# Attention and mixture-of-experts block: P*V of two key tiles together at every second key tile

## The chip, the cores and the metric

The kernel runs on one core of a Trainium2 chip. The time is the device time of one execution in microseconds (us), taken as the median of several runs of the same program. The trace that is read here comes from one profiled execution of the kernel before the change.

## What is computed

The reference is a transformer block on x of 2048 tokens by 256 features: normalise, attention with 16 heads, normalise and add, then a router with 16 experts of which each token takes two, a shared expert, normalise and add. Only the attention is touched. Cut to what matters:

```python
q = (x @ wq); kva = x @ wkv_a; ckv = rmsnorm(kva[..., :64]); k_pe = rope(kva[..., 64:])
k_nope, v = split(ckv @ wkv_b)              # 16 heads
scores = einsum('bhqd,bhkd->bhqk', qs, ks) * scale
scores = where(causal, scores, min)
attn = softmax(scores, axis=-1)
out = einsum('bhqk,bhkd->bhqd', attn, v)    # P*V
y = out.reshape(b, s, H * VD) @ wo
```

The kernel folds wkv_b into the query weights and into wo, so that keys are 128 wide (64 latent and 64 rotary values, the same for all heads) and values are the 64 latent values.

## The kernel before

**Tiling.** Queries are worked in four chunks of 512 (`qc` 0 to 3; here called stages 0 to 3), keys in tiles of 128. Stage `qc` has KT = 4(qc+1) key tiles: 4, 8, 12, 16. The 16 heads are worked in 8 pairs `p`; the two heads of a pair are `s` 0 and 1. A *unit* `i = 2*kt + s` is one head's 128 keys by up to 512 queries, in transposed form; the last four key tiles of a stage lie on the diagonal and have 512, 384, 256 and 128 columns. A pair has U = 2*KT units.

**One unit of scores** (`score_unit`) is three TensorE matmuls in fp16 (lines 1202 to 1204, high and low parts), a fourth (line 1362) that subtracts the row maximum where `row` holds, and one for the causal mask on the diagonal (line 1364). In stages 0 and 1 both heads take the fourth; in stages 2 and 3 only head 0 does, and for head 1 VectorE adds the negated maximum in place (`shift`, line 854). ScalarE then takes the exponential into `Pr` (line 525), a ring of 8 units in SBUF, and GpSimd adds the units up into `Pacc` for the softmax sums (lines 388 and 395). The scores stand in a ring of 4 PSUM banks.

**P*V** (`values(p, kt)`, line 1386) is one fp32 matmul for each head of the pair; each is two passes, so a key tile shows as four instructions. Head 0 writes the lower 64 partitions of one PSUM bank and head 1 the upper 64, all key tiles of a pair adding up there. It waits for the exponentials of its two units; ScalarE may overwrite a slot of `Pr` when P*V and GpSimd have read it.

**Looking ahead.** While pair p is worked, the row maxima of pair p+1 are prepared between the units. `between()` is called three times for each key tile; these calls are counted as *slots*. In slot j < U TensorE makes one *maxima unit* (`max_unit`, line 1333, with a mask matmul at line 1336 on the diagonal) into a ring of two PSUM banks (`MX_RING` is 2), and VectorE reduces it (`maxima`, line 834). Maxima unit j waits on TensorE for the reduction of unit j-2. When half of them are done the maxima are gathered (line 839), turned by TensorE (`turn_max`, line 1345, slots U/2+2 and U+1) and laid out by VectorE (`subtrahend`, line 824). In stages 2 and 3 the maxima of head 1 are then spread over the partitions by TensorE (`spread`, line 1374, slots U+3 and U+5, waiting for `subtrahend`) and copied by VectorE. VectorE also makes the partial sums of the pair before (`part_sums`, line 890) once in each pair but the first, after slot U/4+1. The last pair of a stage prepares nothing. Every engine works its own list in order; VectorE's order in one key tile is: maxima of the first slot, `shift`, maxima of the second and of the third slot.

The order of P*V on TensorE is that of these lines, with LAG = 2:

```python
if kt >= LAG:
    values(p, kt - LAG)
between()
```

and after the loop, the last two key tiles follow directly. So the P*V of key tile kt-2 stands between the second and the third slot of key tile kt, and the last three key tiles of a pair make one unbroken run of P*V. P*V of key tile kt-2 needs the exponentials that the scores of key tile kt have waited for already.

**End of a stage.** TensorE waits for the partial sums of the last pair (`l_done`) before it makes the denominators (line 1439).

Of the kernel before, what the change touches and what calls it, by code (L numbers as in the profile page):

```python
# [53 lines left out]
LAG = 2  # L54
# [18 lines left out]
def attention_moe(nc, x, wq, wkv_a, wkv_b, wo, kv_scale, gate_w, bias, sh_gate, sh_up, sh_down,  # L73
                  ex_gu, ex_down, c32_d, c16_d, out):
    with ExitStack() as ctx:
# [167 lines left out]
        def spread_slots(qc):  # L243

            return (units(qc) + 3, units(qc) + 5) if qc >= SHIFT_FROM else ()
# [15 lines left out]
        def first_unit(qc):  # L261
            return sum(NP * units(q) for q in range(qc))
# [934 lines left out]
        def _(pe):  # L1197
# [88 lines left out]
            for qc in range(NC):  # L1286
# [40 lines left out]
                def max_unit(p, j):  # L1327

                    s, i4, kc = j // (U // 2), j % (U // 2) // (qc + 1), j % (qc + 1)
                    w = CQ if kc < qc else P * (i4 + 1)  # L1330
                    b = 4 + j % MX_RING
                    pe.wait_ge(mx_free, first_unit(qc) + p * U + j + 1)
                    ins = T.matmul(ps[:, b, 0:w], QTh[:, bass.ds((2 * p + s) * CQ + i4 * P, P)],  # L1333
                                   KTh[:, kc * CQ:kc * CQ + w], start=True, stop=(kc < qc))
                    if kc == qc:
                        ins = T.matmul(ps[:, b, w - P:w], identb, mask_qk, start=False, stop=True)
                    ins.then_inc(mx_ready, 1)

                def turn_max(p, s):
                    k = (qc * NP + p) * 2 + s  # L1340
                    pe.wait_ge(m_ready, k + 1)
                    if qc or s or not isinstance(p, int) or p:

                        pe.wait_ge(d_ready, k)
                    T.transpose(ps[0:TC, BK_M, s * P:(s + 1) * P], mrow[:, s, :], ident).then_inc(mt_ready, 1)

                def score_unit(p, i):

                    kt, s = i // 2, i % 2
                    j = kt - TC * qc  # L1350
                    c0 = max(j, 0) * P
                    dst = ps[:, i % ST_RING, c0:]
                    q = bass.ds((2 * p + s) * CQ + c0, CQ - c0)
                    keys = slice(kt * P, (kt + 1) * P)
                    row = s == 0 or qc < SHIFT_FROM
                    if i < 2 and row:
                        pe.wait_ge(d_ready, (qc * NP + p) * 2 + s + 1)

                    pe.wait_ge(exp_done, first_unit(qc) + p * U + i + 1)
                    ins = three(dst, KTh[:, keys], KTl[:, keys], QTh[:, q], QTl[:, q], True, not row and j < 0)  # L1360
                    if row:
                        ins = T.matmul(dst, ones4, Dm[:, p % 2, s, c0:], start=False, stop=(j < 0))  # L1362
                    if j >= 0:
                        ins = T.matmul(ps[:, i % ST_RING, c0:c0 + P], identb, mask_kq, start=False, stop=True)  # L1364
                    ins.then_inc(st_ready, 1)

                def spread(p, h):

                    pe.wait_ge(d_ready, (qc * NP + p) * 2 + 2)
                    k = spreads(qc, p) + h  # L1370
                    if not isinstance(k, int) or k:

                        pe.wait_ge(wide_done, k)
                    T.matmul(ps[:, BK_M, CQ // 2:], ones4, Dm[:, p % 2, 1, h * CQ // 2:(h + 1) * CQ // 2],
                             start=True, stop=True).then_inc(wide_ready, 1)

                def values(p, kt):

                    c0 = max(kt - TC * qc, 0) * P
                    if kt == 0:  # L1380

                        pe.wait_ge(o_free, qc * NP + p + 1)
                    for s in range(2):
                        i = 2 * kt + s
                        pe.wait_ge(exp_done, CR_EXP + first_unit(qc) + p * U + i + 1)
                        T.matmul(ps[LORA * s:LORA * (s + 1), BK_O, c0:], kv[:, kt, 0:LORA],  # L1386
                                 Pr[:, i % P_RING, c0:], start=(kt == 0), stop=(kt == KT - 1)).then_inc(pv_done, 1)

                def pair(p, ahead):

                    slot = 0

                    def between():

                        nonlocal slot
                        if ahead:
                            if slot < U:
                                max_unit(p + 1, slot)
                            if slot == U // 2 + 2:
                                turn_max(p + 1, 0)  # L1400
                            if slot == U + 1:
                                turn_max(p + 1, 1)
                            if slot in spread_slots(qc):
                                spread(p + 1, spread_slots(qc).index(slot))
                            slot += 1

                    for kt in range(KT):
                        score_unit(p, 2 * kt)
                        between()
                        score_unit(p, 2 * kt + 1)  # L1410
                        between()
                        if kt >= LAG:
                            values(p, kt - LAG)
                        between()
                    for kt in range(KT - LAG, KT):
                        values(p, kt)
# [13 lines left out]
                with pe.Fori(0, NP - 1) as p:  # L1430
                    pair(p, True)
                pair(NP - 1, False)


# [188 lines left out]
```

## Time and profile before

| | |
|---|---|
| median of 3 runs | 1482.45 us (1481.38 to 1483.08) |
| span of the profiled execution | 1484.4 us |
| TensorE matmul busy | 1299.4 us, 88% of the span |
| VectorE busy | 935.3 us, 63% |
| GpSimd busy | 851.6 us, 57% |
| ScalarE busy | 644.3 us, 43% |
| mean granted TensorE clock | 0.941 |

The profiled execution has no time of its own beside its span, so its span stands for it; it lies 1.95 us (0.13%) above the median of the runs. Matmuls are pipelined: one of 512 columns is shown as 0.38 us long, though the next starts 0.215 us after it. So starts are to be read, not lengths. "A<-B" names what is written and what is read.

### The profile page before, as it was taken

To read this page: it belongs to the slowest core of one execution; us is meant where nothing else is said; L and a number is where in the kernel's file an instruction comes from. 1 tells how busy PE (TensorE), PEld (TensorE's weight loads), DVE (VectorE), ACT (ScalarE), POOL (GpSimd) and SP (SyncE) were. 2 spreads that over 40 slices of the span, in tenths; PEclk is the share of its full clock that TensorE was granted. 3 is DMA by queue.
4 is the path that set the end of the run, shared out by engine and by line. 5 is a ranking of instruction groups with operands and counts; after the bars stand their busy time and mean duration, and the time that the engine had idled before them with its cause. 6 is when DMAs were issued, how large, how long until landed. Compare 5 with 4: busy or idle time off the path is not lost.

```text
span 1484.4 us, 26542 instructions
## 1 busy us (share of the span) xinstructions
PE 1299.4 (88%) x7260; PEld 634.1 (43%) x7261; DVE 935.3 (63%) x2026; ACT 644.3 (43%) x1321; POOL 851.6 (57%) x900
## 2 busy tenths in 40 slices
PE   3989988899999789999999979999999999868830
PEld 2544564344446423333334632333333333647620
DVE  5555557654534777777663687767777683565536
ACT  3553535244443514444444432444444445347632
POOL 0073426566662747777777364778777778225535
PEclk9999999799999969999999977999999999979975
DMA  8000000000000000000000000000000000046754
GB/s 276 1 1 0 0 15 29 1 0 0 0 0 15 29 1 1 0 0 0 0 0 15 29 22 11 22 21 11 11 21 21 21 11 11 15 112 189 194 143 131
DMA packets 42931, 51.26 MB, mean 35 GB/s; under 512 B 5824, under 2 KB 39744, under 8 KB 42432
## 3 DMA queue, kind: packets, MB, share of 16 engines
q1 hardware_dynamic: 36816, 37.37, 8.1%
q0 software_dynamic: 4864, 10.51, 3.2%
q10 hardware_dynamic: 1200, 2.75, 0.6%
q8 instruction: 26, 0.43, 0.1%
q14 instruction: 25, 0.20, 0.1%
HBM read 35.78 MB, written 14.83 MB: 34 GB/s over the span
## 4 chain that ended last, share of the span: by engine, by line
PE 69%; DVE 13%; issue 6%; POOL 5%; DMA 3%; ACT 3%; DVEq 0%; POOLq 0%; SPq 0%; ACTq 0%
PE ps L1386 17%; PE ps L1202 10%; PE ps L1333 9%; PE ps L1203 9%; PE ps L1204 9%; PE ps L1362 5%; DVE mxp L834 4%; PE ps L1478 2%; DMA B<-xn_rows,tok_i 2%; POOL C L404 1%; DMA B<-in_L_attn_x 1%; POOL A L411 1%; PE ps L1462 1%; POOL C L408 1%; PE ps L1364 1%
## 5 line engine op out<-in xcount | busy, mean ns | idle before, releaser
L395 POOL TENSOR_TENSOR D<-D,B 128x512 f32<-128x512 f32 (+3 forms) x512 | 551.6, 1094 | 118.4 <-ACT B L525 112.7
L525 ACT ACTIVATE B<-ps 128x512 f32<-128x512 f32 (+3 forms) x640 | 335.0, 533 | 530.5 <-DVE ps L854 209.5
L834 DVE TENSOR_REDUCE mxp<-ps 128x1 f32<-128x512 f32 (+3 forms) x640 | 378.5, 605 | 190.6 <-PE ps L1333 130.0
L1386 PE MATMUL ps<-B,kv 128*64 128x512 f32 (+3 forms) x1280 | 290.1, 549 | 0.0
L1333 PE MATMUL ps<-KTh,A 128*128 128x512 f16 (+3 forms) x640 | 233.5, 378 | 27.9 <-DVE mxp L834 18.5
L1202 PE MATMUL ps<-A,KTh 128*128 (+3 forms) x640 | 225.8, 353 | 2.7 <-issue 2.3
L1203 PE MATMUL ps<-A,KTh 128*128 (+3 forms) x640 | 224.6, 351 | 0.0
L1204 PE MATMUL ps<-A,KTl 128*128 (+3 forms) x640 | 223.9, 350 | 0.0
L854 DVE TENSOR_TENSOR ps<-ps,D 128x512 f32<-128x512 f32 x224 | 143.2, 639 | 92.2 <-PE ps L1364 54.9
L388 POOL TENSOR_TENSOR D<-B 128x512 f32<-128x512 f32 (+1 forms) x64 | 76.3, 1199 | 195.8 <-ACT B L525 195.8
L1333 PEld LDWEIGHTS ps<-KTh,A 128*128 (+1 forms) x640 | 62.9, 99 | 227.7 <-issue 118.6
L404 POOL TENSOR_TENSOR C<-C,c 128x128 f32<-128x128 f32 x128 | 62.1, 505 | 169.2 <-ACT C L466 169.2
L1362 PE MATMUL ps<-D,c 128*128 (+4 forms) x416 | 143.7, 345 | 0.0
L466 ACT ACTIVATE C<-ps 128x512 f32<-128x512 f32 (+2 forms) x160 | 81.3, 510 | 97.1 <-PE ps L1204 45.1
L1202 PEld LDWEIGHTS ps<-A,KTh 128*128 128x128 f16 x640 | 62.6, 98 | 107.6 <-issue 72.4
L1386 PEld LDWEIGHTS ps<-B,kv 128*64 128x64 f32 x1280 | 69.9, 135 | 87.5 <-ACT B L525 44.8
L1204 PEld LDWEIGHTS ps<-A,KTl 128*128 128x128 f16 x640 | 63.2, 99 | 57.5 <-issue 2.4
L466 ACT ACTIVATE A<-ps 128x512 f16<-128x512 f32 (+2 forms) x112 | 64.0, 580 | 38.2 <-PE ps L1462 22.3
L1203 PEld LDWEIGHTS ps<-A,KTh 128*128 128x128 f16 x640 | 62.9, 98 | 26.2 <-issue 1.4
L411 POOL DMA_INDIRECT B<-xn_rows,tok_i x48 | 45.4, 947 | 49.1 <-PE ps L1494 48.2
L422 POOL DMA_INDIRECT token_map<-c,where_i x32 | 31.9, 996 | 50.3 <-DVE where_i L998 41.2
L890 DVE TRANSPOSE_TENSOR_REDUCE Lp<-D (+1 forms) x32 | 39.6, 1238 | 32.8 <-POOL D L395 31.3
(209 smaller groups left out, 1793.3 us busy)
## 6 DMA issues: line engine op xcount, KB each, us to landing
results<-B SPq DMA_DIRECT2D x64, 128.0 KB
B<-in_L_attn_x SPq DMA_DIRECT2D x8, 512.0 KB, 4.0
xnTl<-in_L_ffn_experts_gate_up SPq DMA_DIRECT2D x16, 256.0 KB, 2.8
A<-in_L_attn_wq SPq DMA_DIRECT2D x1, 3072.0 KB, 26.0
D<-in_L_attn_wo SPq DMA_DIRECT2D x1, 2048.0 KB, 31.0
xn_rows<-B SPq DMA_DIRECT2D x4, 512.0 KB, 3.0
x_rows<-B SPq DMA_DIRECT2D x4, 512.0 KB, 4.1
xnTl<-in_L_ffn_experts_down SPq DMA_DIRECT2D x16, 128.0 KB, 2.5
```

The source lines that it names most:

```text
L395: nc.gpsimd.tensor_tensor(acc[:, c0:], acc[:, c0:], Pr[:, i % P_RING, c0:], ALU.add).then_inc(sum_done, 1)
L404: ins = nc.gpsimd.tensor_tensor(ropB[:, g % 2, :, dst], pe_of(g)[:, :, src], sine, ALU.mult)
L466: return nc.scalar.activation(dst, src, ACT.Copy, scale=scale)
L525: nc.scalar.activation(Pr[:, i % P_RING, c0:], ps[:, i % ST_RING, c0:], ACT.Exp, scale=SM_SCALE).then_inc(exp_done, 1)
L834: V.tensor_reduce(mxp[:, s, i4, kc:kc + 1], ps[:, 4 + j % MX_RING, 0:w], AX.X, ALU.max).then_inc(mx_free, 1)
L854: V.tensor_tensor(ps[:, i % ST_RING, c0:], ps[:, i % ST_RING, c0:], minus_m[:, p % 2, c0:], ALU.add).then_inc(shifted, 1)
L1202: T.matmul(dst, ah, bh, start=first, stop=False)
L1203: T.matmul(dst, ah, bl, start=False, stop=False)
L1204: return T.matmul(dst, al, bh, start=False, stop=last)
L1333: ins = T.matmul(ps[:, b, 0:w], QTh[:, bass.ds((2 * p + s) * CQ + i4 * P, P)], KTh[:, kc * CQ:kc * CQ + w], start=True, stop=(kc < qc))
L1362: ins = T.matmul(dst, ones4, Dm[:, p % 2, s, c0:], start=False, stop=(j < 0))
L1386: T.matmul(ps[LORA * s:LORA * (s + 1), BK_O, c0:], kv[:, kt, 0:LORA], Pr[:, i % P_RING, c0:], start=(kt == 0), stop=(kt == KT - 1)).then_i ...
```

## The change

P*V is no longer made one key tile at each key tile from kt = 2 on. It is made for two key tiles, kt-3 and kt-2, at each odd kt from 3 on; at even kt there is none. The last two key tiles still follow the loop. No instruction is added or removed on any engine.

```diff
@@ -1409,7 +1409,8 @@
                         between()
                         score_unit(p, 2 * kt + 1)
                         between()
-                        if kt >= LAG:
+                        if kt >= LAG + 1 and kt % 2:
+                            values(p, kt - LAG - 1)
                             values(p, kt - LAG)
                         between()
                     for kt in range(KT - LAG, KT):
```

## Rows read from the trace of the kernel before

**Rows 1.** The page: busy time of TensorE, and the chain that ended last.

```profile
PE 1299.4 (88%) x7260; PEld 634.1 (43%) x7261; DVE 935.3 (63%) x2026; ACT 644.3 (43%) x1321; POOL 851.6 (57%) x900
PE 69%; DVE 13%; issue 6%; POOL 5%; DMA 3%; ACT 3%; DVEq 0%; POOLq 0%; SPq 0%; ACTq 0%
```

**Rows 2.** Busy time by stretch: stage 3, all engines, then granted clock, DMA.

```profile
863.00:1270.00 407.00, 391.77 (x1867) 145.50 (x1866) 287.23 (x478) 173.10 (x299) 301.01 (x264) 0.96 0.06 17
```

**Rows 3.** Timeline of TensorE, stage 3: start, length, instruction, idle before.

```profile
1057.47 0.38 PE L1333 MATMUL ps<-KTh,A 128*128 128x512 f16 x1
1057.78 1.08 PE L1386 MATMUL ps<-B,kv 128*64 128x512 f32 x4
1058.80 0.39 PE L1333 MATMUL ps<-KTh,A 128*128 128x512 f16 x1
```

**Rows 4.** Timeline of TensorE: three key tiles' P*V, stages 1 and 3.

```profile
322.92 1.52 PE L1386 MATMUL ps<-B,kv 128*64 128x384 f32 x12
324.37 0.39 PE L1202 MATMUL ps<-A,KTh 128*128 x1
...
1042.28 1.51 PE L1386 MATMUL ps<-B,kv 128*64 128x384 f32 x12
1044.01 0.39 PE L1202 MATMUL ps<-A,KTh 128*128 x1 [0.22 <-issue]
```

**Rows 5.** Timeline of VectorE, stage 3, at the same place as rows 3.

```profile
1057.68 0.70 DVE L854 TENSOR_TENSOR ps<-ps,D 128x512 f32<-128x512 f32 x1
1058.28 0.68 DVE L834 TENSOR_REDUCE mxp<-ps 128x1 f32<-128x512 f32 x1
1059.22 0.69 DVE L834 TENSOR_REDUCE mxp<-ps 128x1 f32<-128x512 f32 x1 [0.26 <-PE ps L1333]
```

**Rows 6.** Timelines of VectorE and TensorE, stage 3, key tiles 0 and 1.

```profile
1045.30 0.69 DVE L834 TENSOR_REDUCE mxp<-ps 128x1 f32<-128x512 f32 x1 [2.51 <-PE ps L1333]
...
1046.27 0.38 PE L1202 MATMUL ps<-A,KTh 128*128 x1
1047.48 0.23 PE L1333 MATMUL ps<-KTh,A 128*128 128x128 f16 x1 [0.18 <-DVE mxp L834]
```

**Rows 7.** Timelines of TensorE and VectorE, stage 0, key tiles 2 and 3.

```profile
144.83 1.08 PE L1386 MATMUL ps<-B,kv 128*64 128x512 f32 x4
146.13 0.27 PE L1345 MATMUL ps<-c,mrow 128*4 128x128 f32 x1
...
145.81 0.16 DVE L839 TENSOR_REDUCE mrow<-mxp 128x4 f32<-128x4 f32 x1
```

**Rows 8.** Timelines of TensorE and VectorE, stage 1, key tile 2.

```profile
331.20 0.22 PE L1336 MATMUL ps<-c 128*128 128x128 bf16 x1
...
331.25 1.25 DVE L834 TENSOR_REDUCE mxp<-ps 128x1 f32<-128x512 f32 x2
```

**Rows 9.** Timelines of VectorE and TensorE, stage 2, key tiles 2, 3, 8 and 9.

```profile
618.00 1.23 DVE L890 TRANSPOSE_TENSOR_REDUCE Lp<-D  x1
619.16 1.11 DVE L834 TENSOR_REDUCE mxp<-ps 128x1 f32<-128x384 f32 x2
...
619.87 0.38 PE L1333 MATMUL ps<-KTh,A 128*128 128x512 f16 x1
...
637.01 0.67 DVE L824 TENSOR_TENSOR D<-ps,c 4x512 f32 x1
...
638.13 0.27 PE L1374 MATMUL ps<-D,c 128*128 x1
```

**Rows 10.** Timelines of TensorE and VectorE, stage 3, key tiles 4 and 11.

```profile
1056.60 0.39 PE L1333 MATMUL ps<-KTh,A 128*128 128x512 f16 x1
1079.38 0.27 PE L1345 MATMUL ps<-c,mrow 128*4 128x128 f32 x1
...
1078.65 0.17 DVE L839 TENSOR_REDUCE mrow<-mxp 128x4 f32<-128x16 f32 x1
```

**Rows 11.** Timeline of GpSimd, stage 3, last pair.

```profile
1237.58 32.60 POOL L395 TENSOR_TENSOR D<-D,B 128x512 f32<-128x512 f32 x28
```

## The prediction

> **What bounds the kernel now.** I read the page first: TensorE is busy for 88% of the span, and the chain that ended last runs over it for 69%, over VectorE for 13% [rows 1]. The windows by stage come next: in stage 3 TensorE has matmuls for 392 of 407 us, VectorE works 287 and GpSimd 301 us [rows 2]. So inside the pairs of heads TensorE sets the pace, but VectorE has only about 30% to spare, and whether a saving on TensorE arrives must be read from the timelines.
>
> In the regular stretch of stages 2 and 3 (maxima of the next pair being prepared), a 512-column matmul costs 0.215 us from start to start, at a granted clock of 0.96, nearly the 2.4 GHz level. One key tile takes 7 such matmuls of scores and 3 of maxima, 2.15 us, and its P*V. The P*V begins 0.31 us after the maxima matmul ahead of it, 0.095 more than the usual step, and the next matmul starts 1.02 us after it does [rows 3]: 1.11 us in all, 3.27 us for a key tile. VectorE does three reductions of about 0.65 and one shift of 0.60, 2.55 us [rows 5].
>
> **What the change saves.** The same instructions run; only the number of P*V runs falls. Three key tiles in one run, of 384, 256 and 128 columns, cost 1.45 us from first start to next start in stage 1 [rows 4]; one key tile of 512 columns costs 1.02 [rows 3]. The 256 columns of difference cost 0.43, so 512 columns cost 0.86 and each run carries 0.16 that doesn't grow with it; with the 0.095 ahead of it, a run costs 0.25 us beside its columns. P*V of 512 columns added to a run that is there costs 0.86. Joining removes 1, 3, 5 and 7 runs a pair in stages 0 to 3, 128 in all: 32 us if nothing else moved. The bounds of the 0.25: 0.20 if the 0.05 by which a first pass is longer stayed, and 0.30. The Trainium skill (TensorEngine Tiling (Array Packing), Key Properties) says that a change of tiling mode drains TensorE, and P*V is the only work here on half the array's columns; that rule alone promises the whole saving, and rows 3 agree with it in kind.
>
> **What the saving runs into.** P*V at an even key tile was also time for VectorE. Without it, maxima units 1 and 2 of that key tile follow at once, and unit j waits for the reduction of unit j-2. I lay out two key tiles from the first score matmul of the even one. TensorE: scores 0.86; unit 0 at 0.86; scores of head 1 from 1.08; unit 1 at 1.72; unit 2 wanted at 1.94. VectorE may start a reduction 0.42 after its matmul starts [rows 3, 5]: unit 0 from 1.28 to 1.97, shift from 1.93, unit 1 from 2.53 to 3.21; TensorE goes on 0.05 after an end. So unit 2 goes at 2.02 (waits 0.08), the next scores start at 2.24, and unit 3, wanted at 3.10, goes at 3.26 (waits 0.16). With P*V in between, unit 2 went at 3.04 and waited for nothing. The double P*V of the odd key tile then lets VectorE catch up. Sum: -0.25 + 0.24, nothing. The trace shows such key tiles: 0 and 1 of a pair have no P*V, and there unit 2 runs and the next scores start at 1046.27, while the next maxima unit waits until 1047.48, idle for 0.18 and a good 0.3 late [rows 6]. So the waits are real, between 0.24 and 0.44 for an even key tile.
>
> I take 0.24, since key tile 0 alone also waits for the maxima's copy of its own pair; in stage 2, where the third unit is narrow and the next scores come earlier against VectorE, I take 0.05 more.
>
> **Stage 0** (4 key tiles; one P*V moves, from key tile 2 into the closing run). The turn of the second maxima ran at 146.13; the gathering it needs ended at 145.97 [rows 7]. P*V of key tile 0, at 144.83, filled time in which TensorE would have waited for VectorE anyway. After the change that time is idle, the turn starts at about 146.03, and P*V stands in the closing run, for 0.86: +0.86 - 0.10 = +0.75 for each of the 7 pairs that look ahead, **+5.2 us**. The last pair ends with GpSimd's sums: 0.
>
> **Stage 1** (3 runs fewer, -0.75 a pair; no shift, so VectorE has time). One place costs: the partial sums occupy VectorE until 331.25, then come the reductions of units 6 and 7. Unit 8 needs that of unit 6, done about 331.9; TensorE would be there at 331.26, once P*V at 331.35 is gone [rows 8]. It waits about 0.7, which eats the 0.75: six pairs at 0. The first pair has no partial sums, -0.75; the last lies between -0.75 and 0 (GpSimd's sums end it), taken at -0.45. **-1.2 us.**
>
> **Stage 2** (5 runs fewer). Key tiles 2 and 3: the partial sums run from 618.00, unit 8 is reduced from 619.16 for about 0.52, and unit 10 needs it: 619.74, as against 619.87 before [rows 9], when one P*V was already done that now still has to run. Unit 11 came at 621.19; now it is 619.74 + 0.215 + 0.095 + 1.87 for two P*V = 621.92: +0.73. Key tiles 4 to 7: +0.1. Key tile 9: the spread of the maxima waits for `subtrahend`, 637.01 to 637.68; before it ran at 638.13 with P*V ahead of it [rows 9], now it goes at about 637.8, the scores behind it likewise, and the double P*V follows: +0.6. Key tiles 10 and 11: -0.25. In the closing run the last P*V waits for the last exponential: 1.73 us in stage 3 against 1.45 in stage 1 [rows 4]. With a fourth key tile ahead of it that wait is covered: -0.28 in stages 2 and 3. Sum +0.9 for six pairs; the first, without partial sums, +0.2; the last is GpSimd's, 0. **+5.6 us.**
>
> **Stage 3** (7 runs fewer). Key tiles 2 to 5: maxima unit 12 already waits behind the partial sums before (at 1056.60, 0.3 late [rows 10]); the moved P*V makes that wait useful: -0.25 - 0.3, less 0.2 of new waits, -0.35. Key tiles 6 and 7: `subtrahend`, 0.6, comes ahead of shift and unit 19, so unit 21 waits 0.38: +0.2. Key tiles 8 and 9: 0. Key tiles 10 and 11: the turn needs the gathering, done at 1078.82, and ran at 1079.38 [rows 10]; without P*V at key tile 10 it would be due at 1078.27 and waits 0.6: +0.35. Key tiles 12 to 15: no maxima are left, -0.5. Closing run -0.28. Sum -0.58 for six pairs; the first -0.3. In the last pair GpSimd adds for 32.6 us without a pause [rows 11], which TensorE can't shorten: 0. **-3.8 us.**
>
> Nothing else is late. Exponentials: `Pr` holds four key tiles and P*V of kt-4 is still issued ahead of the scores of kt. ScalarE and GpSimd get their work in the same order, and no DMA depends on where in a pair P*V stands.
>
> **Sum:** 5.2 - 1.2 + 5.6 - 3.8 = +5.8 us on the profiled execution's 1484.4, 1490.2. The median of the runs is 1.95 lower: **1488 us**, 0.4% slower.
>
> **The rivals.** A measurement of this kernel can tell about 0.2%, 3 us, from no change.
> (1) *Forecast:* the waits eat the saving and a little more; +3 to +9 us. Chance 0.48.
> (2) *A draw:* the same terms, with errors of 0.05 us each over 60 double key tiles (3 us), and 0.03 on each of 128 joinings (4 us), of which a part cancels. Within 3 us of before. 0.27.
> (3) *Faster:* the waits behind VectorE at four places (stage 0's turn, partial sums in stages 1 and 2, the spread) are shorter than laid out, because VectorE's own list moves up when TensorE arrives earlier. These places hold 5.2 + 0.75 x 6 + 0.98 x 6 + 0.85 x 7 = 22 us. Where less than 13 us of it appear, the sum is below -3. If half does, 1477 us. Against it: in all four VectorE is busy back to back on work that doesn't wait for the moved P*V. 0.12. That the whole 32 us arrive (1450 us) I hold at 0.03. It is what the drain rule of the Trainium skill (TensorEngine Tiling (Array Packing), Key Properties) would give by itself; it has no say on VectorE.
> (4) *Clearly slower:* an even key tile costs the 0.44 seen at the start of a pair, not 0.24 [rows 6]. There are 2 such double key tiles a pair in stage 2 and 2 in stage 3, besides those costed above; 0.2 x 30, and waits that spill into the third: +12 us, 1494. 0.10.
>
> Range: (1), (2) and most of (3) and (4), 1477 to 1496; the forecast's own is 1485 to 1492. Faster by over 0.2%: 0.15; within: 0.27; slower: 0.58.
>
> **What would show it.** Right: in the changed trace P*V stands as eight instructions of 512 columns with 1.87 us to the next start; the idle time of maxima units on TensorE "waiting for VectorE" (line 1333) and of the turn (line 1345) grows by 20 us or more; a pair of stage 0 takes 0.75 longer, one of stage 2 0.9 longer, one of stage 3 0.6 less; stages 0 and 2 lose, 1 and 3 gain. VectorE's, ScalarE's and GpSimd's busy times stay. Wrong: a double run costs 2.0 us or more (then all is about 16 us slower than laid out), or the start of `score_unit` is held by exponentials, which I have at nowhere.

## The result, and the profile after

The changed kernel takes **1494.22 us** (median of four runs, 1492.94 to 1495.68), the kernel before beside it 1482.53. The ratio is 1.0076, with a 95% interval of 1.0062 to 1.0090: slower by 0.8%. Slower was forecast, at 1488; the time lies within the range given, 6 us above the forecast and above the 1485 to 1492 that the forecast's own case allowed.

The page of the changed kernel, its busy times and the chain that ended last, against [rows 1]; under them the groups of the maxima's matmul (line 1333) and of its weight load:

```profile
span 1491.0 us, 26535 instructions
PE 1285.3 (86%) x7260; PEld 649.9 (44%) x7261; DVE 933.9 (63%) x2026; ACT 633.5 (42%) x1321; POOL 846.0 (57%) x900
PE 61%; DVE 15%; issue 9%; POOL 6%; ACT 4%; DMA 3%; DVEq 1%; POOLq 0%; ACTq 0%; SPq 0%
...
L1333 PE MATMUL ps<-KTh,A 128*128 128x512 f16 (+3 forms) x640 | 229.9, 378 | 35.8 <-DVE mxp L834 25.2
L1333 PEld LDWEIGHTS ps<-KTh,A 128*128 (+1 forms) x640 | 62.9, 99 | 219.4 <-DVE mxp L834 123.8
```

TensorE is busy for 14 us less with the same 7260 matmuls, its share of the chain falls from 69% to 61%, and yet the kernel takes longer. The last column says where the time went. The matmul's idle time that ended with a reduction is 25.2 us, against 18.5 on the page of before. That of the weight load ahead of it is 123.8, against 64.5 (in the kernel before the two together have 83.0, here 148.9).

The double P*V itself does what was laid out. Timeline of TensorE, stage 3, eight P*V instructions and what follows:

```profile
1044.26 1.94 PE L1386 MATMUL ps<-B,kv 128*64 128x512 f32 x8
1046.13 0.28 PE L1374 MATMUL ps<-D,c 128*128 x1
```

The next start is 1.87 us behind, 0.86 more than behind one key tile [rows 3]. The unrounded starts of such a run are 938.775, 938.781, 939.255, 939.261 and so on, in twos 6 ns apart, and only the third and the fourth raise the semaphore that tells of a head's P*V. So the two heads, on the lower and the upper 64 partitions of the bank, run side by side, and each step takes 0.43 us, two of the 0.215 of an fp16 matmul. A head is not two passes of 0.215 that follow those of the other head, as the text before the prediction can be read; the 0.86 for a key tile stands.

The clock is also as before: the windows give stage 3 a granted clock of 0.96, as in [rows 2], for nearly the same matmuls (1863, there 1867):

```profile
878.00:1280.00 402.00, 382.55 (x1863) 150.03 (x1860) 286.15 (x475) 167.59 (x298) 298.31 (x261) 0.96 0.06 17
```

**Reading it by pairs.** In a stage the pairs between the first and the last are alike to 0.05 us or so (two exceptions in the kernel before are named further down), and an instruction that stands once in each pair shows their length. Timeline of TensorE: the closing run of P*V in stage 0, the first turn of the maxima in stage 2, the second turn in stage 3, each in two successive pairs.

```profile
148.67 2.37 PE L1386 MATMUL ps<-B,kv 128*64 128x512 f32 x16
160.26 2.38 PE L1386 MATMUL ps<-B,kv 128*64 128x512 f32 x16
...
702.97 0.27 PE L1345 MATMUL ps<-c,mrow 128*4 128x128 f32 x1
738.72 0.27 PE L1345 MATMUL ps<-c,mrow 128*4 128x128 f32 x1
...
1089.69 0.27 PE L1345 MATMUL ps<-c,mrow 128*4 128x128 f32 x1 [0.45 <-DVE mrow L839]
1135.98 0.27 PE L1345 MATMUL ps<-c,mrow 128*4 128x128 f32 x1 [0.45 <-DVE mrow L839]
```

11.59, 35.75 and 46.28 us (the last from unrounded starts). The first instruction behind the closing run of P*V, read in this way in every stage, gives this table. "Rest" is the first pair of the stage together with the work ahead of it.

| us | stage 0 | stage 1 | stage 2 | stage 3 | sum |
|---|---|---|---|---|---|
| regular pair, before | 10.73 | 22.36 | 34.68 | 46.86 | |
| regular pair, after | 11.59 | 22.40 | 35.75 | 46.28 | |
| difference, forecast | +0.75 | 0 | +0.9 | -0.58 | |
| difference, measured | +0.86 | +0.04 | +1.07 | -0.58 | |
| six pairs | +5.1 | +0.3 | +6.7 | -3.2 | +8.9 |
| last pair | 0 | -0.6 | -0.2 | +1.6 | +0.8 |
| rest | +1.1 | -1.5 | +1.5 | -0.3 | +0.8 |
| stage, measured | +6.3 | -1.9 | +8.1 | -1.9 | +10.6 |
| stage, forecast | +5.2 | -1.2 | +5.6 | -3.8 | +5.8 |

The denominators of stage 3 start at 1282.09 us, against 1271.51 before, 10.6 later. Behind them nothing was changed, but that stretch takes 212.9 us in the execution of before and 208.9 here, so the spans differ by only 6.6, while the medians differ by 11.7. In the other kernels below it takes 207.7 to 212.5 us. Where a profiled execution has a time of its own, that is 1.9 us more than its span (here 1492.94 and 1491.0). By that the execution of before, with a span of 1484.4, stands for about 1486.3 and was 3.8 us above the median of its runs, not 1.95, and the one here 1.3 below: 5.1 us, which is what the difference of the spans lacks. The forecast's difference of +5.8 doesn't depend on this. Attention's 10.6 is the number to set beside 11.7.

**The places.** Stage 0, timelines of TensorE and then VectorE, against [rows 7]:

```profile
145.60 0.33 PE L1333 MATMUL ps<-KTh,A 128*128 128x384 f16 x1 [0.96 <-DVE mxp L834]
145.83 0.27 PE L1345 MATMUL ps<-c,mrow 128*4 128x128 f32 x1
148.02 0.27 PE L1345 MATMUL ps<-c,mrow 128*4 128x128 f32 x1 [0.82 <-DVE mrow L839]
...
144.04 1.25 DVE L890 TRANSPOSE_TENSOR_REDUCE Lp<-D  x1 [0.24 <-issue]
147.10 0.67 DVE L834 TENSOR_REDUCE mxp<-ps 128x1 f32<-128x512 f32 x1
147.81 0.16 DVE L839 TENSOR_REDUCE mrow<-mxp 128x4 f32<-128x4 f32 x1
```

The gathering ends at 147.97 and the turn goes at 148.02, 0.05 behind it; TensorE has stood idle for 0.82 us where P*V used to be. Stage 2, timelines of VectorE and TensorE in a regular pair, against [rows 9]:

```profile
625.03 1.24 DVE L890 TRANSPOSE_TENSOR_REDUCE Lp<-D  x1
626.19 1.12 DVE L834 TENSOR_REDUCE mxp<-ps 128x1 f32<-128x384 f32 x2
644.95 0.67 DVE L824 TENSOR_TENSOR D<-ps,c 4x512 f32 x1
...
626.77 0.39 PE L1333 MATMUL ps<-KTh,A 128*128 128x512 f16 x1 [0.47 <-DVE mxp L834]
627.09 1.94 PE L1386 MATMUL ps<-B,kv 128*64 128x512 f32 x8
645.82 0.28 PE L1374 MATMUL ps<-D,c 128*128 x1 [0.70 <-DVE D L824]
```

Both waits that were laid out are there. The maxima unit behind the partial sums waits for its reduction, and two key tiles' P*V still have to run behind it. The spread waits 0.70 us for `subtrahend`.

**The place I had at nothing.** The last pair of stage 3, timelines of VectorE, GpSimd, ScalarE and TensorE, against [rows 11]:

```profile
1264.84 0.70 DVE L854 TENSOR_TENSOR ps<-ps,D 128x512 f32<-128x512 f32 x1 [2.79 <-PE ps L1204]
1265.45 5.24 DVE L898 SCALAR_TENSOR_TENSOR WEl<-xnTl,WEh 128x768 f16<-128x768 f32 x1
1270.61 1.28 DVE L854 TENSOR_TENSOR ps<-ps,D 128x512 f32<-128x512 f32 x2
1273.34 0.96 DVE L898 SCALAR_TENSOR_TENSOR WEl<-xnTl,WEh 128x768 f16<-128x768 f32 x1
...
1246.51 23.36 POOL L395 TENSOR_TENSOR D<-D,B 128x512 f32<-128x512 f32 x19
1272.21 8.54 POOL L395 TENSOR_TENSOR D<-D,B 128x512 f32<-128x512 f32 x9 [2.34 <-ACT B L525]
...
1271.46 1.96 ACT L525 ACTIVATE B<-ps 128x512 f32<-128x512 f32 x4 [3.94 <-DVE ps L854]
...
1272.11 0.34 PE L1202 MATMUL ps<-A,KTh 128*128 128x384 f16 x1 [1.50 <-ACT B L525]
```

VectorE's cut of an expert's weights (`cut_expert`, line 898: it makes the low fp16 half of an expert's weights, work for a later part of the kernel that is done here in between) takes 5.24 us at first and 0.96 eight microseconds later. It ends only when GpSimd, which has added without a pause for 23.36 us, has run out of exponentials. The shift behind it is late, so ScalarE is idle for 3.94, GpSimd for 2.34 and TensorE for 1.50. GpSimd sets the end of this pair, and the pair is 1.63 us longer.

### The profile page after: what moved, and what is told of

The parts are those of the page before. It is cut to its first block, busy times and chain, and to the rows that moved or that the text cites. A ratio compares the mean times of both kernels' runs of the same rounds, so it can differ in the third digit from the quotient of the medians.

```text
span 1491.0 us, 26535 instructions
## 1 busy us (share of the span) xinstructions
PE 1285.3 (86%) x7260; PEld 649.9 (44%) x7261; DVE 933.9 (63%) x2026; ACT 633.5 (42%) x1321; POOL 846.0 (57%) x900
## 4 chain that ended last, share of the span: by engine, by line
PE 61%; DVE 15%; issue 9%; POOL 6%; ACT 4%; DMA 3%; DVEq 1%; POOLq 0%; ACTq 0%; SPq 0%
PE ps L1386 15%; PE ps L1202 8%; PE ps L1333 8%; PE ps L1204 8%; PE ps L1203 8%; DVE mxp L834 4%; PE ps L1362 4%; PE ps L1479 2%; DMA B<-xn_rows,tok_i 1%; DMA B<-in_L_attn_x 1%; POOL C L404 1%; PE ps L1463 1%; POOL D L388 1%; POOL C L408 1%; POOL A L411 1%
## 5 line engine op out<-in xcount | busy, mean ns | idle before, releaser
L525 ACT ACTIVATE B<-ps 128x512 f32<-128x512 f32 (+3 forms) x640 | 324.9, 533 | 520.9 <-DVE ps L854 182.4
L834 DVE TENSOR_REDUCE mxp<-ps 128x1 f32<-128x512 f32 (+3 forms) x640 | 372.3, 604 | 209.6 <-PE ps L1333 127.8
L1386 PE MATMUL ps<-B,kv 128*64 128x512 f32 (+3 forms) x1280 | 261.9, 538 | 0.0
L1333 PE MATMUL ps<-KTh,A 128*128 128x512 f16 (+3 forms) x640 | 229.9, 378 | 35.8 <-DVE mxp L834 25.2
L1333 PEld LDWEIGHTS ps<-KTh,A 128*128 (+1 forms) x640 | 62.9, 99 | 219.4 <-DVE mxp L834 123.8
L1386 PEld LDWEIGHTS ps<-B,kv 128*64 128x64 f32 x1280 | 80.5, 136 | 126.1 <-issue 100.5
```

Of the source, the lines that this page charges most:

```text
L525: nc.scalar.activation(Pr[:, i % P_RING, c0:], ps[:, i % ST_RING, c0:], ACT.Exp, scale=SM_SCALE).then_inc(exp_done, 1)
L834: V.tensor_reduce(mxp[:, s, i4, kc:kc + 1], ps[:, 4 + j % MX_RING, 0:w], AX.X, ALU.max).then_inc(mx_free, 1)
```

## Experiments

Theory: what a joining gives or costs is decided by what VectorE has to do at that place; where VectorE has nothing pressing, it saves 0.25 us. The main rival is that a longer P*V costs of itself.

**e1: stage 0 as before.**

```diff
-                        if kt >= LAG + 1 and kt % 2:
+                        if qc == 0:
+                            if kt >= LAG:
+                                values(p, kt - LAG)
+                        elif kt >= LAG + 1 and kt % 2:
```

> Stage 0 has P*V where it was before, stages 1 to 3 stay joined. If P*V of key tile 0 filled a wait for VectorE's gathered maxima, a pair of stage 0 takes 10.73 us again instead of 11.59, the pairs of stages 1 to 3 stay at 22.40, 35.75 and 46.28, and the time falls by 7 x 0.86 = 6 us against the changed kernel, to about 1488. Rival (the loss comes from joining as such, wherever it is): the pairs of stage 0 gain no more than the others, 1 to 2 us in all.

Measured: 1489.33 us, ratio to before 1.0034 (1.0022 to 1.0045). A pair of stage 0 takes 10.73 us again, and the regular pairs of the other stages stay where they were: 22.40, 35.75, 46.28. The stages can be read one by one, and stage 0 carries 6 us of the loss (1.0076 less 1.0034 is 6.2 us, and seven pairs at 0.86 are 6.0).

**e2 and e3: partial sums later,** in the changed kernel and in the one before.

```diff
-                    if slot == U // 4 + 1 and sums is not None:
+                    if slot == (10, 18, 32, 38)[qc] and sums is not None:
```

> The changed kernel, with the partial sums of the pair before moved on VectorE behind the last maxima (slots 10, 18, 32 and 38). If maxima units wait because the partial sums hold VectorE, unit 8 of stage 1 and units 9 and 10 of stage 2 no longer wait: a pair of stage 1 goes from 22.40 to about 21.7, one of stage 2 from 35.75 to about 35.0, stage 3 changes by less than 0.2, and stage 0 gets shorter too, because its maxima end 1.2 us earlier: about 10.8. Together -15 us against the changed kernel. Rival (VectorE is only late by its steady load): no stage moves by more than 0.2 a pair.

> The kernel before with the same move of the partial sums, as the control of the run before it. If the places are as read, stage 1 (22.36) and stage 2 (34.68) don't change, since there P*V hid the partial sums; stage 3 falls by the 0.3 that maxima unit 12 waits; stage 0 falls by up to 1 us a pair, where unit 6 waits behind the partial sums. -5 to -10 us. Rival: every stage gains as much as the changed kernel does from it.

Measured: the changed kernel with late sums 1481.20 us (0.9980 of before, 0.9967 to 0.9994); the kernel before with late sums 1473.41 (0.9923, 0.9907 to 0.9940). Regular pairs of e2: 10.45, 21.59, 35.46, 46.28; of e3: 9.63, 22.36, 34.63, 46.55. So in stage 1 a joined pair is now 0.77 us shorter than a plain one, which is three runs at 0.25, where it was 0.04 longer: there the partial sums had eaten the whole saving. In stage 2 the wait at key tiles 2 and 3 went (0.65 us), but slot 32 of 36 was a poor choice: the closing run took 0.36 more (2.67 us, not 2.31), so that only 0.29 of the gain was left, 35.46 where 35.0 was expected. That the sums there delay the last shifts is my reading. The gain of 1.1 us a pair in stage 0 that e3 shows is not in the prediction: in the short pair the 1.25 us of partial sums lie on VectorE's way to the second turn, joined or not. The loss by joining stays in stage 0 even so: 10.45 against 9.63.

**e4: join only behind the last maxima.** The kernel before, with one joining a pair in stages 1 and 2 and two in stage 3, all in the last quarter of a pair.

```diff
+                def joined(kt):
+                    return qc > 0 and kt % 2 == 1 and kt < KT and kt - 1 >= 3 * KT // 4
+
...
-                        if kt >= LAG:
+                        if joined(kt):
+                            values(p, kt - LAG - 1)
+                        if kt >= LAG and not joined(kt + 1):
                             values(p, kt - LAG)
```

> Joined only where no maxima unit is left: at the last odd key tile of stages 1 and 2, at the last two of stage 3, not in stage 0. If a run of P*V costs 0.25 beside its columns and nothing waits there, the pairs take 10.73, 22.36 - 0.26 = 22.10, 34.68 - 0.56 = 34.12 and 46.87 - 0.79 = 46.08; 8 x 0.26 + 7 x 0.56 + 7 x 0.79 = 11.5 us faster than before, 1471. Rival (the saving is lost on other engines): within 3 us of before.

Measured: 1474.42 us, ratio 0.9935 (0.9918 to 0.9951). Pairs: 10.73, 22.10, 34.12, 46.09. Each joining is worth 0.25 or 0.26, and the fourth key tile in the closing run about 0.3 more in stages 2 and 3, as the prediction had priced them. Joining gains 0.65% where VectorE has no maxima to reduce.

**e5 and e6: short reductions,** in the changed kernel and in the one before. Part of the maxima is left out (a reduction reads the first 128 columns only), so that VectorE is done early with all of them.

```diff
-                V.tensor_reduce(mxp[:, s, i4, kc:kc + 1], ps[:, 4 + j % MX_RING, 0:w], AX.X,
+                V.tensor_reduce(mxp[:, s, i4, kc:kc + 1], ps[:, 4 + j % MX_RING, 0:min(w, 128)], AX.X,
```

> The changed kernel with every reduction of row maxima (line 834) reading only the first 128 columns of its unit, so that VectorE needs about 0.29 us instead of 0.69 for each; the maxima are those of a part of the keys. To be read beside the same edit of the kernel before. If VectorE's pace ate the saving, the changed kernel is now ahead: against that control a pair of stage 1 takes about 0.4 less, of stage 2 about 0.7 less (the turn and the spread still wait), of stage 3 about 1.9 less, and of stage 0 about 0.45 more. Rival (the joined P*V costs TensorE time by itself): the differences stay at +0.86, +0.05, +1.07 and -0.58.

> The kernel before with the same short reductions, as the control. TensorE sets its pace in stages 1 to 3, so the pairs should change little: about 22.35, 34.6 and 46.4; stage 0, where TensorE waits behind VectorE, falls by about 0.5 from 10.73. Rival (VectorE sets the pace before the change too): all stages fall by more than 1 us a pair.

Measured (one run each): the changed kernel 1429.80 us, the one before 1444.61. The sign turns: with the same TensorE work in both, joining is now 14.8 us *faster*. Regular pairs 10.64, 21.52, 33.60, 44.15 joined, against 10.27, 22.29, 33.88, 45.90. The granted clock in stage 3 is 0.99 in both. In stage 1 the difference is -0.77, three runs at 0.26. In stage 3 it is -1.75, which looks like seven runs at 0.25 but isn't: by the starts of the key tiles, 2 and 3, 4 and 5, 8 and 9, and 12 and 13 give 0.26 each, 6 and 7 give 0.16, 10 and 11 give 0.04, and 14 and 15 with the closing run 0.51, of which 0.25 is the wait in the closing run that a fourth key tile covers. So where nothing waits a run does cost 0.25 us beside its columns, and a double run costs nothing of its own. In stages 0 and 2 the difference is +0.37 and -0.28, against -0.25 and -1.25. This edit shortens neither the partial sums nor `subtrahend`: key tiles 8 and 9 of stage 2 still lose 0.72.

**e7: spread later,** in the changed kernel, by two slots.

```diff
-            return (units(qc) + 3, units(qc) + 5) if qc >= SHIFT_FROM else ()
+            return (units(qc) + 5, units(qc) + 7) if qc >= SHIFT_FROM else ()
```

> The changed kernel with the two spreads of the maxima moved two slots later (to U+5 and U+7). If TensorE waits at the first of them for VectorE's layout in key tile 9 of stage 2, that wait goes: a pair of stage 2 falls from 35.75 to about 35.0 (0.7 less); stages 0, 1 and 3 stay at 11.59, 22.40 and 46.28. Rival (the wait belongs to the double P*V behind it): stage 2 stays at 35.75.

Measured: 1494.03 us (one run), where the pairs expected would have given 4 us less: a miss. A pair of stage 2 takes 35.28, 0.47 less and not 0.7, so that the wait for `subtrahend` was there to be had. But a pair of stage 3 takes 46.94, 0.66 more. Timelines of TensorE and VectorE in stage 3:

```profile
1090.96 0.27 PE L1374 MATMUL ps<-D,c 128*128 x1
1092.33 0.28 PE L1374 MATMUL ps<-D,c 128*128 x1 [0.39 <-DVE D L844]
...
1091.16 0.70 DVE L854 TENSOR_TENSOR ps<-ps,D 128x512 f32<-128x512 f32 x1 [2.38 <-PE ps L1364]
1091.77 0.41 DVE L844 COPY D<-ps 128x256 f32 x1
```

The second spread writes the bank that VectorE copies out after the first. In the new place the first spread comes just ahead of a shift's turn on VectorE; the copy has to stand behind that shift, ends at 1092.18, and TensorE, done with the scores about 0.55 earlier than it may go on, waits for it. I had asked what the second spread gives, not what the first one meets.

**e8: the cut in the last pairs with one input from SBUF.** In the changed kernel; the low half of the experts' weights is left out there.

```diff
+                if one:
+                    V.tensor_scalar(WEl[:, e, :], stage[:, 1 - r, :], WS, 0.0, ALU.mult, ALU.add).then_inc(raw_lo, 1)
+                    return
```

> The changed kernel, where in the last pair of a stage the two VectorE operations that make the low half of an expert's weights (line 898) read one SBUF tensor instead of two; the low half is left out there. In the changed kernel the first of them took 5.24 us instead of 0.96 while GpSimd added without a pause, and the last pair of stage 3 took 41.97 instead of 40.34. If two SBUF inputs are what is shut out by GpSimd, the operation takes about 1 us here and the last pair about 40.3. Rival (VectorE is held by something else, or any operation of that size would be): it stays near 5 us and 41.9.

Measured: 1497.46 us (one run); the last pair of stage 3 takes 41.20, not 41.97, nor the 40.34 of before. VectorE:

```profile
1267.16 4.87 DVE L899 TENSOR_SCALAR WEl<-xnTl 128x768 f16<-128x768 f32 x1
1274.68 0.56 DVE L899 TENSOR_SCALAR WEl<-xnTl 128x768 f16<-128x768 f32 x1
```

The operation is fast (0.56 us, 1.4 elements a nanosecond in each partition, against 0.8 of the other form) and is shut out just as long. So a second input from SBUF is not needed for it; the expectation failed. The Trainium skill (SBUF — State Buffer, Who interferes with whom) says that VectorE shares a pair of ports with GpSimd, and contends for it in an operation with two SBUF inputs and in the fast two-port modes, which a `tensor_scalar` can enter. The trace agrees with both in kind, 5.24 and 4.87 us; it doesn't show the mode itself, only the higher speed.

**e11: no cut in the last pair.** In the changed kernel; VectorE cuts the last two experts after the last partial sums of stage 3.

```diff
-                    if qc == NC - 1 and kt in (KT - 6, KT - 3):
+                    if qc == NC - 1 and ahead and kt in (KT - 6, KT - 3):
...
                 part_sums(qc, NP - 1)
+                if qc == NC - 1:
+                    cut_expert(NP - 1, 0)
+                    cut_expert(NP - 1, 1)
```

> The changed kernel, but VectorE cuts the low halves of the last pair's two experts after the last partial sums of stage 3, not inside that pair. Theory (the cut is shut out while GpSimd adds from a backlog without a pause, and the shift behind it is late): without an operation of that kind in the pair, GpSimd has no pause of 2.3 us, and the last pair of stage 3 takes 40.35 us, as before, not 41.97; the cuts then take 1.8 to 1.9 us behind the sums, of which up to that much lies on VectorE's way to the reciprocal, so the whole gains 0 to 1.6 us. Rival (the last pair is longer because of the order of P*V in it): 41.97 stays.

Measured: 1490.40 us, ratio to before 1.0045 (1.0030 to 1.0061), against 1.0076 with the cuts inside. The last pair takes **38.88** us, 3.1 less than in the changed kernel and 1.5 less than before. GpSimd, then VectorE:

```profile
1248.59 31.15 POOL L395 TENSOR_TENSOR D<-D,B 128x512 f32<-128x512 f32 x28
...
1279.77 1.25 DVE L890 TRANSPOSE_TENSOR_REDUCE Lp<-D 128x32 f32<-128x1024 f32 x1 [2.85 <-POOL D L395]
1280.94 1.78 DVE L898 SCALAR_TENSOR_TENSOR WEl<-xnTl,WEh 128x768 f16<-128x768 f32 x2
```

The pause is gone, and more than that: the same 28 additions take 31.15 us, not the 32.60 of [rows 11]. In the kernel before, the two of them that meet the cuts took 1.89 us (shown at the end) and, with 384 columns,

```profile
1265.32 1.71 POOL L395 TENSOR_TENSOR D<-D,B 128x384 f32<-128x384 f32 x1
```

and in e11 the same two take 1.29 and 1.02. So about 1.3 of the 1.45 us is GpSimd waiting for the cuts: they also cost in the kernel before, only there GpSimd paid. I expected 40.35 and had missed this half. The rest of the 1.45 isn't separated, since e11 differs from the kernel before in the order of P*V too.

**e12: only the last pair of stage 3 as before.**

```diff
-                        if kt >= LAG + 1 and kt % 2:
+                        if qc == NC - 1 and not ahead:
+                            if kt >= LAG:
+                                values(p, kt - LAG)
+                        elif kt >= LAG + 1 and kt % 2:
```

> The changed kernel, but in the last pair of stage 3 P*V of one key tile at each key tile, as before. Theory (in the changed kernel TensorE runs ahead of GpSimd in this pair, which gives GpSimd a backlog of exponentials to add, and with a backlog it makes no gap for VectorE): with the old order of P*V the copies come as they came before, the cut takes 1.8 us or less and the pair 40.35 us. Rival (the backlog comes from the pairs before, which are 0.58 us shorter each): the cut again takes about 5 us and the pair about 42.

Measured: 1492.18 us (one run); the pair takes 40.33 us, and the cut

```profile
1267.83 1.76 DVE L898 SCALAR_TENSOR_TENSOR WEl<-xnTl,WEh 128x768 f16<-128x768 f32 x1
```

So it is the order of P*V inside this pair, and not what the earlier pairs leave behind, that shuts VectorE out. The other kernels agree: the first cut of this pair takes 5.24 or 5.25 us in e1, e2, e5 and e7, where the whole pair is joined, and 1.72 to 1.77 in e3, e4, e6, e9 and e10, where nothing is joined in it ahead of key tile 13.

**e9 and e10: the two findings together.** The kernel before with late sums (slot 26 in stage 2) and P*V joined only where it pays; e10 joins in stage 1 at the last place alone.

```diff
-                    if slot == U // 4 + 1 and sums is not None:
+                    if slot == (10, 18, 26, 38)[qc] and sums is not None:
...
+                    return qc == 1 and kt % 2 == 1 and 3 <= kt < KT or qc > 1 and kt % 2 == 1 and kt < KT and kt - 1 >= 3 * KT // 4
```

> The kernel before with the partial sums moved as in the runs with late sums (slots 10, 18, 26 and 38), P*V of two key tiles joined at all odd key tiles of stage 1, only at key tile 11 in stage 2, only at 13 and 15 in stage 3, nowhere in stage 0. Theory (what a joining is worth is decided by VectorE's list at its place, and the places add up): pairs of 9.63, 21.59, 34.1 and 45.8 us, against 10.73, 22.36, 34.68 and 46.86: 3.5 us over the four stages, times six pairs, 21 us, and another 2 us from last pairs: about 1459 us. Rival (the two edits share the same slack and don't add): no more than the late sums alone gave, about 1473.

> As the run before this one, but stage 1 joins only at its last odd key tile. Theory: a pair of stage 1 takes 22.1 us and the others stay (9.63, 34.1, 45.8), so the whole is 3 us slower than the other, 1462. Rival: joinings early in a pair of stage 1 are worth nothing, 1459.

Measured: e9 **1459.66 us**, ratio 0.9847 (0.9834 to 0.9861), pairs of 9.63, 21.59, 34.12, 45.78 and a last pair of 40.34. e10 1465.23 us, ratio 0.9877 (0.9862 to 0.9892), with 22.10 in stage 1. The places add up, and e9 beats both kernels; the late sums alone (e3) had given half of its gain. e10 came out 5.6 us behind e9, where its pairs explain 3.3. In the profiled executions the rest lies in stretches whose code is the same in both (3.1 us more up to the end of the first pair, 2.0 more after attention), and these vary as much between the other kernels.

## Why the prediction came out so

**Right: the mechanism and the sign.** A run costs 0.25 us beside its columns (e4, e5 against e6) and a double run costs 1.87. The saving arrives at five of seven joinings in stage 3 as soon as the reductions are quick, and the sign of the change turns with VectorE's time alone. The saving is eaten at places that the timeline of before showed. What the 0.25 consists of, the drain that the prediction names or something else, no run here separates.

**The signs.** The idle time of line 1333 that ended with a reduction grew by 66 us with its weight loads (83.0 to 148.9) and by 6.7 without them, that of the turn by 17 (16.5 to 33.3); more than the 20 us asked for, though nearly all of line 1333's stands at the weight loads. Stages 0 and 2 lost, 1 and 3 gained. ScalarE's busy time did not stay: 644.3 to 633.5 us, with as many instructions and the mean exponential at 533 ns in both, so that they only overlap more.

**Stage 0, +0.75: measured +0.86.** The P*V of 0.86 was priced rightly. The 0.10 that I counted as won, because the turn could go earlier, did not arrive: the turn stands 0.10 earlier in the pair, but the closing run starts 9.28 us into it, against 9.29 before. That the short score matmuls between the two were paced by TensorE's own queue is my reading; no run tested it.

**Stage 1, 0: measured +0.04.** The wait behind the partial sums is there, 0.82 us (key tiles 2 and 3 come out at +0.56, not -0.26), and e2 against e3 shows -0.77 without it.

**Stage 2, +0.9: measured +1.07.** By place, forecast and measured: key tiles 2 and 3, +0.73 and +0.74; 4 to 7, +0.1 and +0.17; 8 and 9, +0.6 and +0.72; the rest, -0.53 and -0.56. The spread is the term mis-sized: it goes 0.2 us behind the end of `subtrahend` (645.62), where I had allowed 0.1.

**Stage 3, -0.58: measured -0.58.** By place: key tiles 2 to 5, -0.35 and -0.30; 6 and 7, +0.2 and +0.14; 8 and 9, 0 and 0; 10 and 11, +0.35 and +0.36; the rest, -0.78 and -0.79.

**Wrong: "In the last pair GpSimd adds for 32.6 us without a pause [rows 11], which TensorE can't shorten: 0."** It can be lengthened. This was +1.6 us, because "VectorE's busy times stay" and "Nothing else is late" were wrong for one instruction of VectorE. I had checked who sets the end of that pair but not which of VectorE's operations meet GpSimd's additions there. e11 and e12 show that the cut and the order of P*V in this pair make the loss together. The row of [rows 11] looked like an engine at its limit, and about 1.3 us of it was waiting for VectorE.

**The rest of the gap.** Attention lost 10.6 us, not 5.8. Of the difference, 1.6 lie in that last pair, less 0.4 for the last pairs of stages 1 and 2, which gained more than laid out (-0.6 and -0.2, not -0.45 and 0). The regular pairs of stages 0 to 2 give 1.9 (0.11, 0.04 and 0.17, six times each). Another 0.6 comes from the seventh pairs of stages 2 and 3, which took 34.38 and 46.60 us before, 0.3 less than the others, and so had less to gain; I had treated them as the others. The last 1.0 stands in the first pairs and ahead of them, +0.8 in all where I had -0.1. For that part I have no cause: in stage 1 this stretch takes 99.7 us in the changed kernel and 101.3 in e1, whose code is the same there.

**The rivals.** The draw and the faster case fell: the four places of (3) hold the time that was laid out for them or more, and VectorE's list did not move up. Rival (4) gave the right time, 1494, mostly for a wrong reason: an even key tile in the steady stretch costs not 0.44 but 0.26 in stage 3, where key tiles 8 and 9 come out at 0, and 0.34 in stage 2, where 4 to 7 lose 0.08 a joining.

## What to carry to other kernels

Before work on the bounding engine is gathered into longer runs, ask at each place what the second engine does in the gap that closes: here one edit gave -1.5% together with a move of the second engine's own work (e9) and +0.8% when made everywhere. Read gains by the length of a repeated unit (a pair) and by stage; that resolved 0.05 us where a whole run shows 3. And an engine that "works without a pause" may be waiting inside its instructions: compare the mean time of one with the same instruction elsewhere before it is called the bound.

## What the runs showed of the hardware

A VectorE operation that meets GpSimd can be passed over several times. Timeline of GpSimd in the changed kernel, from 0.5 us before the cut of 5.24 us began; then the addition of the kernel before that followed the cut of 1.76 us at 1257.54:

```profile
1264.91 4.96 POOL L395 TENSOR_TENSOR D<-D,B 128x512 f32<-128x512 f32 x4
```

```profile
1258.55 1.89 POOL L395 TENSOR_TENSOR D<-D,B 128x512 f32<-128x512 f32 x1
```

In the first case three more additions, at 1266.13, 1267.37 and 1268.60, start after the cut, 1.23 us apart and each 1.28 long, so that they overlap, and all of them are finished before it. Their exponentials were done 1.1 to 1.8 us ahead: GpSimd had a stock. e8 has the same picture with a cut at 1267.16 and additions at 1267.87, 1269.10 and 1270.33. In the second case GpSimd's next input came only at 1258.4; its addition at 1257.19 ended, the cut went through, and the next addition took 1.89 us, 0.6 more than usual.

It is tempting to say that a stock keeps VectorE out and a gap lets it in. Other cuts of the changed kernel refute that. The second cut of the last pair starts at 1273.34 and takes 0.96; the next addition's exponential had been done since 1272.54, and here GpSimd waited. Its addition; then, in the pair before, VectorE's cut and GpSimd's additions:

```profile
1273.45 1.99 POOL L395 TENSOR_TENSOR D<-D,B 128x512 f32<-128x512 f32 x1
...
1235.15 1.75 DVE L898 SCALAR_TENSOR_TENSOR WEl<-xnTl,WEh 128x768 f32 x1
...
1234.82 2.94 POOL L395 TENSOR_TENSOR D<-D,B 128x512 f32<-128x512 f32 x2 [0.29 <-ACT B L525]
```

There GpSimd goes from one addition to the next without a pause, its input ready 0.10 us before the cut began, and the cut still gets in after one addition. So what decides whether VectorE waits for one addition or for four stays open. The Trainium skill (SBUF — State Buffer, Who interferes with whom) says that the one that issues first gets the shared ports for the whole instruction and that the other blocks. Blocking is as shown, on both sides (5.24 us here, 1.99 for GpSimd), but the first cut began ahead of three additions and still came last.
